# Taps and decays of a long convolution: four blocks in one transfer each, from tables with time on the partitions

## The chip, the cores and the metric

The kernel runs on one core of a Trainium2 chip. The metric is the device time of one execution in microseconds, the median of three runs. The engines are named as in the profile: PE does the matmuls (PEld its weight loads), DVE and POOL elementwise work, ACT activations and copies, SP issues most of the DMAs. SPq and ACTq are the queues' own issuing instructions.

## The reference

Two layers with a residual each. The first is a long convolution along time for each of 512 channels, the second a routed low-rank FFN on the first 4096 tokens (of batch 0).

```python
# x: (8, 4096, 512), float32; N = 16 states for each channel
x = x + conv(_layernorm(x))
x = x + ffn(_layernorm(x))

# conv
p, a = sigmoid(delta), sigmoid(alpha)
q = 1.0 - p * a
kernel = p * beta * jnp.exp(t * jnp.log(q))                     # (512, 16, 4096)
k = jnp.einsum('dnl,dn->dl', kernel, gamma * scale)             # taps, (512, 4096)
out = irfft(rfft(xt, n=2*l) * rfft(k, n=2*l))[..., :l] + x * omega

# ffn: for each expert e, tokens gathered by index, output scattered with weights
h = gelu(xr @ w1A[e].T @ w1B[e]);  ye = h @ w2A[e].T @ w2B[e]
```

## The kernel before

Time is cut into 32 chunks of 128 steps. Within a chunk the convolution is a 128 x 128 triangular Toeplitz matrix for each channel (`local`, L1568), and what earlier chunks add goes through 16 states for each channel (`chunk`, L1553; a scan on DVE, L1380; `between`, L1580). Channels go in **units** of 8 and **blocks** of two units (16 channels, `KD`). There are 32 blocks for each half of the batch, so 64 blocks and 128 units. A **tile** is 8 blocks (128 channels) of 128 rows of x, 8 MB, loaded and stored in 16 pieces.

The span has five parts: the start, in which SP streams x for the layer norm's sums while PE and ACT build tables (0 to 117 us); the first half of the batch (to about 374 us); the FFN (to about 785 us); the second half (to 1047 us); and the last stores.

The **tables** are built at the start, one block at a time (`table`, L948 on ACT and L1531 on PE). For a block, ACT makes two exponentials (L953). PE multiplies them into 4 x 512 numbers of taps, with channel pairs on the partitions and time along the row, and transposes them. ACT copies taps (L961) and decays (L963) out of PSUM and issues a DMA for each (L969, L971) to `decay_d` and `taps_d` in HBM.

In the **blocks**, taps and decays come back block by block. SP's `load_weights` (L777) issues one DMA of 256 KB for the taps (32 partitions, each shifted by one step, eight rows of 256 numbers) and one of 128 KB for the decays. Four blocks of taps lie in `wide`, in four groups of 32 partitions, and four of decays in `dk`. Each pair is issued three blocks ahead, when ACT has turned and POOL has placed the block before the present one (`s_rev`, `s_wd`). Between the pairs SP issues the loads of the next tile and the stores of the last one (`tile`, L800).

ACT's program for a unit is five instructions (`steps`, L1000): an exponential (L1008), a scaled copy of the chunk sums (L1012), two reversals that turn taps in time into the Toeplitz matrix `wb` (L1031, 1024 numbers on each of 32 partitions; L1032, 768), and a copy to the lower partitions (L1038). A row of `wide` holds time with the two channels of a pair side by side, so the reversal reads every second number, backwards: steps of 8 bytes. It writes `wb` without gaps. Only block 0 of the second half is turned by DVE (`reverse2`, L1461), because ACT is in the FFN then.

POOL centres half of a unit (L625) and copies decays to `near` (L574). DVE centres the other half (L1342), scales (L1353), scans (L1380) and adds the result to x (L1364). Each engine runs its program in order, and semaphores count units.

Of the kernel before, what the change touches and what calls it, by code (L numbers as in the profile page):

```python
# [48 lines left out]
def build(nc, x, delta, alpha, beta, gamma, omega, ew, ei, w1a, w1b, w2a, w2b, out, ei_experts=8):  # L49
# [20 lines left out]
    TB = 4  # L70
    WB = 4
    NL = P // LR
# [40 lines left out]
    with ctx:  # L113
# [18 lines left out]
        wide = sb("wide", [P, 2 * UC * P])  # L132
# [17 lines left out]
        om = sb("om", [P, NU, 2])  # L150
        eps = sb("eps", [P, 1])
        root = sb("root", [P, 2])
        lag = sb("lag", [P, 2, 2 * D])
        spare = sb("spare", [P, 4])


# [35 lines left out]
        tok_x = wide[:].rearrange("p (k h d) -> p k h d", k=2, h=2)  # L192
        turned_taps = wide[0:SB // 2, :].rearrange("p (h k i d) -> p h k i d", h=TB, k=2, d=2)
        taps_in = wide[:].rearrange("p (s m) -> p s m", s=SB)
# [13 lines left out]
        out_lag = lag[:].rearrange("p k (h d) -> p k h d", h=2)  # L208
# [4 lines left out]
        carry_row = carry[:].rearrange("p k c -> p (k c)")  # L213
        hot = carry_row[:, 0:3 * E * TT].rearrange("p (k e j) -> p k e j", k=3, e=E)
# [29 lines left out]
        slots_l = lag[0:NSC, 0, 0:2 * P].rearrange("c (p w) -> c p w", w=2)  # L244
# [22 lines left out]
        s_tapd = [sem(f"s_tapd{k}") for k in range(TB)]  # L267
        s_dk = [sem(f"s_dk{k}") for k in range(WB)]
# [9 lines left out]
        s_w = [sem(f"s_wk{k}") for k in range(WB)]  # L278
# [145 lines left out]

        def joined(t):

            return t % DG == 1
# [6 lines left out]
        def _(pool):  # L434
# [8 lines left out]
            const(pool.memset(om[:], 0.0))  # L443
# [124 lines left out]
            def place_decays(i):  # L568

                dst = near[:, i % 2][:, :, 0:3:2, :]  # L570
                src = dk[:, i % WB].rearrange("p (n s d) -> p s d n", s=SB, d=2)
                wait(pool, s_loc, 2 * (i - 1))
                wait(pool, s_dk[i % WB], 16 * (i // WB + 1))
                pool.tensor_copy(dst, src).then_inc(s_wd, 1)  # L574
# [145 lines left out]
        def _(sp):  # L720
# [33 lines left out]
            sp.dma_start(om[0:SB // 2], omega.rearrange("(u s d) -> s u d", d=2, s=SB // 2)).then_inc(s_om, 16)  # L754
# [5 lines left out]
            sp.dma_start(taps_d.rearrange("k s i d -> (k s) i d")[:, P:P + ZR, :]  # L760
                         .rearrange("(a p) i d -> p a (i d)", p=P), zero).then_inc(s_tab, 16)
# [10 lines left out]
            for k in range(TB):  # L772
                sp.wait_ge(s_tapd[k], 16 * (NK // TB))
            sp.wait_ge(s_dec, 16 * NK)
            sp.wait_ge(s_tab, 16)

            def load_weights(i, k):  # L777

                kb = i % NK if isinstance(i, int) else sp.snap(i % NK)
                row = taps_d[bass.ds(kb, 1)].rearrange("k s i d -> k (s i d)")  # L780
                dec = decay_d[bass.ds(kb, 1)].rearrange("k s n d -> (k s) (n d)")
                turned, placed = 2 * (i - WB + 1), i - WB + 1
                now(sp, turned, placed)
                wait(sp, s_rev, turned)
# [3 lines left out]
                wait(sp, s_wd, placed)  # L788
                if isinstance(i, int) and NK <= i < NK + WB:
                    sp.wait_ge(s_dn, grp(NP))  # L790
                sp.dma_start(dk[:, k, :], dec).then_inc(s_dk[k], 16)
# [66 lines left out]
            def tiles(g):  # L858
                t0 = g * DG
                if g == 0:  # L860
                    for k in range(1, WB):
                        load_weights(k, k)
# [53 lines left out]
            for k in range(WB):  # L916
                load_weights(NK + k, k)
# [8 lines left out]
            for k in range(2):  # L926
                sp.wait_ge(s_s[2 * k], 16 * ((NQ + 1 - k) // 2))
                sp.wait_ge(s_s[2 * k + 1], 16 * (NP // 2))
# [6 lines left out]
        def _(act):  # L935
# [20 lines left out]
            def table_copied(i):  # L956
# [3 lines left out]
                wait(act, s_tapd[i % TB], 16 * (i // TB))  # L960
                act.activation(turned_taps[:, i % TB].rearrange("p k i d -> p k d i"),  # L961
                               ps[0:SB // 2, 4 * h, :].rearrange("p (k d i) -> p k d i", k=2, d=2), ACT.Copy)
# [3 lines left out]
            def table_out(i):  # L966

                act.wait_ge(s_cp, i + 1)
                act.dma_start(decay_d[i].rearrange("s n d -> s (n d)"),  # L969
                              decays[:, i].rearrange("p n d -> p (n d)")).then_inc(s_dec, 16)  # L970
                act.dma_start(taps_d[i, :, 0:P, :].rearrange("(k s) i d -> s k (i d)", k=2),  # L971
                              turned_taps[:, i % TB].rearrange("p k i d -> p k (i d)")).then_inc(s_tapd[i % TB], 16)

            act.wait_ge(s_const, NCONST)
            for i in range(NK):
# [3 lines left out]
                if i > 1:  # L979
                    table_out(i - 2)  # L980
            table_copied(NK - 1)
            table_out(NK - 2)
# [808 lines left out]
```

## Time and profile before

| | us |
|---|---|
| median of 3 runs | 1080.95 |
| the runs | 1082.27, 1079.19, 1080.95 |
| the profiled execution | 1070.18 |
| its span, first to last instruction | 1068.0 |
| busy in the span: PE, DVE, ACT, POOL | 869.4, 816.4, 761.4, 571.5 |
| mean granted clock of PE | 0.94 |

The shares of busy time are means over five parts with different limits, so each part is read by itself. The profile's groups give, for a line of the code and a shape, the count, the busy time, the mean duration and the idle time of the engine just before; the waits say what ended such idle time; the timeline gives single instructions.

### The profile page before, as it was taken

The numbers are of one execution on the slowest core, as the hardware profiler recorded it, in microseconds if no ns is written. First come the engines' busy times: TensorE is split into PE (matmuls) and PEld (weight loads), VectorE is DVE, ScalarE is ACT, GpSimd is POOL, SyncE is SP. The second block draws the span as 40 slices with busy tenths as digits, with TensorE's granted clock in tenths as the row PEclk, the third lists the DMA queues.
The fourth block names the chain that finished last, engine by engine and source line by source line (L and its number), as shares of the span: only waits on it lengthen the run. The fifth ranks groups of instructions, "written<-read, shape, count | busy, mean of one in ns | idle before, by whom it ended". The sixth has DMA issues, their size and how long they took to land.

```text
span 1068.0 us, 31991 instructions
## 1 busy us (share of the span) xinstructions
PE 869.4 (81%) x11186; PEld 730.9 (68%) x11186; DVE 816.4 (76%) x1350; ACT 761.4 (71%) x1124; POOL 571.5 (54%) x641
## 2 busy tenths in 40 slices
PE   2770588887868969999999999997878889786981
PEld 1550477776757758888888888886757777675771
DVE  7988899987969834577777777775689998797891
ACT  3882599997969756566665665664459999696990
POOL 5444788867857232666666656655553333332330
PEclk9995699998989979999999999999989999898996
DMA  8999899999999979999999999899669999999977
GB/s 300 351 400 385 211 264 209 271 266 295 308 279 285 327 182 309 257 293 318 286 312 259 242 268 244 246 256 240 174 157 268 226 252 281 287 296 300 295 159 158
DMA packets 390529, 286.11 MB, mean 268 GB/s; under 512 B 124784, under 2 KB 338434, under 8 KB 389948
## 3 DMA queue, kind: packets, MB, share of 16 engines
q1 hardware_dynamic: 345980, 211.67, 72.6%
q0 software_dynamic: 17952, 34.42, 14.6%
q10 hardware_dynamic: 26528, 39.14, 10.4%
q8 instruction: 39, 0.64, 0.3%
q14 instruction: 30, 0.25, 0.1%
HBM read 195.57 MB, written 98.77 MB: 276 GB/s over the span
## 4 chain that ended last, share of the span: by engine, by line
PE 31%; issue 17%; ACT 15%; DVE 14%; DMA 13%; POOL 3%; SPq 2%; DVEq 1%; ACTq 1%; POOLq 0%
PE ps L1688 8%; DMA xb<-L_attn_x 6%; PE ps L1714 6%; ACT wb L1032 6%; DVE xb L1364 4%; ACT wb L1038 4%; PE ps L1562 4%; PE ps L1575 3%; PE ps L1587 3%; DMA wide<-y_d,slot_g 3%; ACT carry L1008 3%; DVE wb L1182 2%; PE ps L1650 2%; PE ps L1663 2%; DVE state L1380 2%
## 5 line engine op out<-in xcount | busy, mean ns | idle before, releaser
L1575 PE MATMUL ps<-xn,wb 128*128 128x128 f32 x2048 | 273.0, 288 | 0.0
L1575 PEld LDWEIGHTS ps<-xn,wb 128*128 128x128 f32 x2048 | 248.0, 198 | 17.0 <-issue 2.3
L625 POOL TENSOR_TENSOR cen<-xb,mean 128x512 f32<-128x512 f32 x128 | 142.8, 1119 | 217.0 <-DVE state L1380 144.2
L1353 DVE TENSOR_TENSOR xn<-cen,rstd 128x1024 f32<-128x1024 f32 x128 | 177.1, 1384 | 44.9 <-POOL cen L625 36.1
L1140 ACT ACTIVATE cen<-ps 128x1024 f32<-128x1024 f32 x110 | 109.2, 1023 | 101.6 <-PE ps L1688 64.7
L1562 PE MATMUL ps<-xn,near 128*32 128x128 f32 x2048 | 87.5, 291 | 113.0 <-DVE xn L1353 67.9
L1364 DVE TENSOR_TENSOR xb<-xb,ps 128x1024 f32 (+1 forms) x128 | 152.7, 1193 | 7.6 <-PE ps L1587 7.6
L1031 ACT ACTIVATE wb<-wide 32x1024 f32<-32x1024 f32 x126 | 144.5, 1147 | 15.4 <-DMA wide<-taps_d 12.9
L1562 PEld LDWEIGHTS ps<-xn,near 128*32 128x32 f32 x2048 | 52.6, 113 | 137.2 <-issue 72.1
L1688 PE MATMUL ps<-carry,wb 64*128 64x256 f32 x1024 | 126.8, 388 | 7.7 <-DVE carry L1426 4.6
L1688 PEld LDWEIGHTS ps<-carry,wb 64*128 64x128 f32 x1024 | 99.4, 190 | 37.1 <-issue 18.5
L1195 DVE BATCH_NORM_STATS2 xb<-xb 128x512 f32 (+1 forms) x128 | 84.3, 684 | 45.3 <-DMA xb<-L_attn_x 45.1
L1032 ACT ACTIVATE wb<-wide 32x768 f32<-32x768 f32 x126 | 114.8, 911 | 1.5
L505 POOL DMA_INDIRECT slot_d<-rowf,posi x64 | 106.1, 1658 | 11.9 <-issue 11.9
L1342 DVE TENSOR_TENSOR cen<-xb,mean 128x512 f32<-128x512 f32 x128 | 90.2, 705 | 9.3 <-DMA xb<-L_attn_x 9.2
L1714 PE MATMUL ps<-cen,xn 128*64 128x128 f32 x1536 | 96.4, 275 | 0.0
L1587 PE MATMUL ps<-state,carry 32*128 32x128 f32 x2048 | 93.6, 297 | 0.0
L1182 DVE BATCH_NORM_STATS2 wb<-xb 128x512 f32 (+1 forms) x128 | 79.8, 681 | 15.7 <-DMA xb<-L_attn_x 14.5
L1714 PEld LDWEIGHTS ps<-cen,xn 128*64 128x64 f32 x1536 | 84.3, 137 | 5.3 <-issue 5.1
L1587 PEld LDWEIGHTS ps<-state,carry 32*128 32x128 f32 x2048 | 69.2, 186 | 25.9 <-issue 25.1
L1038 ACT ACTIVATE wb<-wb 64x512 f32<-64x512 f32 x128 | 80.5, 629 | 4.9 <-DVE wb L1466 1.8
L1008 ACT ACTIVATE carry<-far,rate 128x384 f32<-128x384 f32 x128 | 79.0, 617 | 3.2
(211 smaller groups left out, 1311.4 us busy)
## 6 DMA issues: line engine op xcount, KB each, us to landing
xb<-L_attn_x SPq DMA_DIRECT2D x160, 512.0 KB, 7.4
out<-xb SPq DMA_DIRECT2D x72, 512.0 KB, 6.4
xb<-L_attn_x ACTq DMA_DIRECT2D x128, 256.0 KB, 5.8
out<-xb SPq DMA_DIRECT2D x88, 256.0 KB, 4.7
wb<-L_ffn_w_B SPq DMA_DIRECT2D x78, 256.0 KB
wide<-taps_d SPq DMA_DIRECT2D x63, 256.0 KB, 5.8
dk<-decay_d SPq DMA_DIRECT2D x63, 128.0 KB, 5.6
out<-y_d SPq DMA_DIRECT2D x4, 1536.0 KB, 11.6
```

The lines of the kernel that those rows point to most:

```text
L625: pool.tensor_tensor(cen[:, k, 0:QB // 2].rearrange("p b r d -> p r b d"), unit_view(pool, g, i, k)[:, :, 0:UC // 2] .rearrange("p r (b d) ...
L1008: act.activation(carry[:, k, 0:CR + P], far[:], ACT.Exp, scale=rate[:, bass.ds(col, 1)])\
L1031: act.activation(dst[0:ZR], src, ACT.Copy)
L1032: act.activation(dst[ZR:2 * ZR, :, :, ZR:P], src[:, :, :, 0:P - ZR], ACT.Copy).then_inc(s_rev, 1)
L1038: act.activation(taps[2 * ZR:P, :, :, 2 * ZR:P], taps[0:2 * ZR, :, :, 0:2 * ZR], ACT.Copy)\
L1353: dve.tensor_tensor(xn[:, k].rearrange("p (b d) r -> p b d r", d=2), cen[:, k].rearrange("p b r d -> p b d r"), rstd[:, g * P:(g + 1) * P] ...
L1364: dve.tensor_tensor(view, view, ps[:, QB * k:QB * k + QB, 0:2 * P] .rearrange("p b (d r) -> p r b d", d=2), ALU.add).then_inc(s_ev, 1)
L1562: ins = pe.matmul(ps[b * 2 * N:(b + 1) * 2 * N, QB * k, 2 * P:3 * P], near[:, h, k * QB + b, d:d + 2, :].rearrange("p z n -> p (z n)"), xn ...
L1575: ins = pe.matmul(ps[:, QB * k + b, d * P:(d + 1) * P], wb[:, h, k * QB + b, d, :], xn[:, k, 2 * b + d, :], start=(b > 0 and d == 0), stop ...
L1587: ins = pe.matmul(ps[:, QB * k + b, d * P:(d + 1) * P], carry[rows, k, d * P:(d + 1) * P], state[rows, k, :], start=False, stop=True, skip ...
L1688: ins = pe.matmul(ps[:, 2 * (b % 2) + h, f * QT:(f + 1) * QT].rearrange("p (a t) -> p a t", a=2), w1bs[half_rows, k, c * P:(c + 1) * P], r ...
L1714: ins = pe.matmul(ps[h * RANK:(h + 1) * RANK, 4, 0:P], w2as[:, (f // 2) * (FC // 2) + 2 * b + f % 2, :], act_at(q, b)[:, f, side * P:(side ...
```

## The change

Taps in HBM are now laid out as `taps_d[block, time, 16 channels]`, decays as `decay_d[group of four blocks, state, 4 x 256]`. On PE the roles in the table's matmul are swapped: the exponential is the stationary operand and the 8 coefficient columns move, so the result has time on 128 partitions and 16 channels along the row. ACT's copy of the taps is 128 x 16 in place of 4 x 512. The DMAs that write the tables are issued once for four blocks.

One DMA now loads the taps of four blocks: 128 partitions, each one run of 2048 numbers (8 KB), 1 MB in all. One loads their decays, 512 KB. Both have two buffers: `taps_in[:, 0:2]`, the second half of which is the old `lag` buffer, and `dk` with `dk_odd` (inside `carry`). SP still waits for `s_rev` and `s_wd` at each block, since its other DMAs are paced by them, but issues taps and decays twice for each tile.

A row of `taps_in` holds time with 16 channels side by side. The reversal on ACT reads one channel of them backwards in time: its innermost step is 16 numbers, 64 bytes. It writes `wb` as before, and its instructions have the shapes that they had.

Because `lag` holds the FFN's last results until the scatter has read them, SP waits for all scatters (`scattered`) before the first load into it in the second half.

```diff
-        taps_d = nc.dram_tensor("taps_d", [NK, SB, P + ZR, 2], F32).ap()
-        decay_d = nc.dram_tensor("decay_d", [NK, P, N, KD], F32).ap()
+        taps_d = nc.dram_tensor("taps_d", [NK, P + ZR, KD], F32).ap()
+        decay_d = nc.dram_tensor("decay_d", [NG, P, WB * N * KD], F32).ap()
...
+        def taps_of(q, n, k):
+            return taps_in[q * ZR:(q + 1) * ZR, n, :].rearrange("p (i c) -> p i c", c=KD)[:, ::-1, k * UC:(k + 1) * UC]\
+                .rearrange("p m (s d) -> p s d m", d=2)
...
-                src = bass.AP(row.tensor, row.offset, [[2, ZR], [2 * (P + ZR), SB], [1, 2 * P]])
-                sp.dma_start(taps_in[k * ZR:(k + 1) * ZR], src).then_inc(s_w[k], 16)
...
+            def load_taps(n, k0=0):
+                wait(sp, s_rev, 2 * WB * (n - 1))
+                wait(sp, s_w, 16 * n)
+                first = taps_d[n % NG * WB + k0]
+                src = bass.AP(first.tensor, first.offset, [[(P + ZR) * KD, WB - k0], [KD, ZR], [1, P * KD]])
+                sp.dma_start(taps_in[k0 * ZR:, n % 2, :], src).then_inc(s_w, 16)
...
-                        load_weights(t * BT + b + WB - 1, (b + WB - 1) % WB)
+                        wait(sp, s_rev, 2 * (t * BT + b))
+                        wait(sp, s_wd, t * BT + b)
+                    if b == (1 if first else 0):
...
+                        load_taps(2 * t + 1)
+                        load_decays(2 * t + 1)
+                    elif b == WB and not final:
+                        load_taps(2 * t + 2)
+                        load_decays(2 * t + 2)
...
             def reverse(i, k, m):
-                src = taps_in[m * ZR:(m + 1) * ZR, k * QB:(k + 1) * QB].rearrange("p s (m d) -> p s d m", d=2)[:, :, :, ::-1]
+                src = taps_of(m % WB, m // WB, k)
...
-                    for d in range(2):
-                        pe.matmul(o[:, k, d, :], own_coef[:, u, d::2], decay[:, 2 * h + k, :],
-                                  start=(k == 0 and d == 0), stop=False, skip_group_check=True)
+                    pe.matmul(ps[:, 4 * h, k * UC:(k + 1) * UC], decay[:, 2 * h + k, :], own_coef[:, u, :],
+                              start=(k == 0), stop=False, skip_group_check=True)
```

Two places show the order. The first is SP at the end of the second tile of the first half: pieces of the next tile are loaded (`xb<-L_attn_x`), taps and decays of coming blocks fetched. Before:

```order
L732 DMA xb<-L_attn_x 128x8x128
L787 DMA wide<-taps_d 32x8x256
L791 DMA dk<-decay_d 128x256
L851 DMA out<-xb 128x8x64
L732 DMA xb<-L_attn_x 128x8x128 x4
L787 DMA wide<-taps_d 32x8x256
L791 DMA dk<-decay_d 128x256
L787 DMA wide<-taps_d 32x8x256
L791 DMA dk<-decay_d 128x256
L749 DMA y_d<-xb 128x8x128 x4
```

and with the change:

```order
L886 DMA out<-xb 128x8x64
L750 DMA xb<-L_attn_x 128x8x128
L886 DMA out<-xb 128x8x64
L750 DMA xb<-L_attn_x 128x8x128 x4
L801 DMA taps_in<-taps_d 128x1x2048
L807 DMA carry<-decay_d 128x1024
L767 DMA y_d<-xb 128x8x128 x4
L750 DMA xb<-L_attn_x 128x8x128
```

Three pairs of DMAs have become one pair of four blocks' size, and the four loads of x no longer stand behind one.

The second is ACT in the first unit of a half. Before:

```order
L1008 ACTIVATE carry<-far,rate 128x384
L1012 ACTIVATE shift_s<-ps,coef 128x4x31
L1031 ACTIVATE wb<-wide 32x1024
L1032 ACTIVATE wb<-wide 32x8x96
L1038 ACTIVATE wb<-wb 64x8x64
```

and with the change:

```order
L1035 ACTIVATE carry<-far,rate 128x384
L1039 ACTIVATE shift_s<-ps,coef 128x4x31
L1061 ACTIVATE wb<-taps_in 32x1024
L1062 ACTIVATE wb<-taps_in 32x8x96
L1068 ACTIVATE wb<-wb 64x8x64
```

Nothing moves: the same five instructions of the same shapes stand in the same order, with other names and line numbers (L1061 and L1062 are the reversals). The loop over them is written for eight blocks in place of four.

## Rows read from the trace of the kernel before

**Rows 1.** Groups of ACT's instructions, 120 to 374 us: busy, mean ns, idle before.

```profile
L1031 ACT ACTIVATE wb<-wide 32x1024 f32<-32x1024 f32 x62 | 71.2, 1149 | 1.4
L1032 ACT ACTIVATE wb<-wide 32x768 f32<-32x768 f32 x62 | 56.5, 912 | 0.7
L1038 ACT ACTIVATE wb<-wb 64x512 f32<-64x512 f32 x63 | 39.6, 629 | 1.5
L1008 ACT ACTIVATE carry<-far,rate 128x384 f32<-128x384 f32 x63 | 38.9, 617 | 1.6
L1012 ACT ACTIVATE shift_s<-ps,coef 128x124 f32<-128x124 f32 x64 | 22.7, 355 | 23.6 <-PE ps L1562 23.2
```

**Rows 2.** The same groups, 785 to 1047 us.

```profile
L1012 ACT ACTIVATE shift_s<-ps,coef 128x124 f32<-128x124 f32 x64 | 22.7, 355 | 25.3 <-PE ps L1562 24.6
```

**Rows 3.** Windows: PE, PEld, DVE, ACT, POOL busy (instructions), granted clock, DMA, GB/s.

```profile
140.00:160.00 20.00, 17.89 (x254) 15.21 (x252) 18.80 (x23) 19.53 (x28) 17.87 (x14) 1.00 1.10 258
...
740.00:760.00 20.00, 14.01 (x172) 11.97 (x171) 12.78 (x30) 6.98 (x11) 11.47 (x11) 0.91 1.03 260
```

**Rows 4.** Waits of ACT, 120 to 374 us: total, times, longest.

```profile
ACT shift_s L1012 <- PE ps L1562: 23.2, 10, 7.9
```

**Rows 5.** Waits of ACT, whole span.

```profile
ACT wb L1031 <- DMA wide<-taps_d: 12.9, 1, 12.9
```

**Rows 6.** Groups of all engines, whole span.

```profile
L574 POOL COPY near<-dk 128x256 f32<-128x256 f32 x64 | 40.2, 628 | 0.0
...
L1083 ACT ACTIVATE xn<-ps 128x512 f32<-128x512 f32 x64 | 34.8, 595 | 4.3 <-PE ps L1650 4.2
...
L497 POOL COPY xb<-xb 128x256 f32<-128x256 f32 x64 | 25.4, 403 | 41.3 <-DMA xb<-L_attn_x 40.5
...
L963 ACT ACTIVATE xb<-ps 128x256 f32<-128x256 f32 x32 | 18.3, 573 | 0.0
...
L1120 ACT ACTIVATE xb<-wb 128x256 f32 x39 | 16.3, 417 | 49.1 <-PE ps L1663 24.3 <-DVE xb L1208 17.1 <-issue 6.7
...
L1226 DVE TENSOR_TENSOR rstd<-rstd 128x128 f32<-128x128 f32 x2 | 0.6, 286 | 0.0
...
L1228 DVE TENSOR_TENSOR rstd<-rstd,xb 128x128 f32<-128x128 f32 x1 | 0.4, 387 | 0.0
```

**Rows 7.** One line's instructions, L1465 and L1466: ns min/median/max.

```profile
L1465 DVE COPY wb<-wide x2: 681/1882/3084, 782.9 to 786.6; 32x1024 f32<-32x1024 f32 x2
...
L1466 DVE COPY wb<-wide x2: 549/549/549, 786.0 to 787.3; 32x768 f32<-32x768 f32 x2
```

**Rows 8.** Timeline at the tile boundary, 229 to 247 us: start, us, engine, instruction, [idle].

```profile
229.32 6.67 SPq L732 DMA_DIRECT2D xb<-L_attn_x  x4
...
234.18 0.64 PE L1562 MATMUL ps<-xn,near 128*32 128x128 f32 x16 [0.17 <-DVE xb L1364]
...
235.41 2.05 PE L1575 MATMUL ps<-xn,wb 128*128 128x128 f32 x16
...
237.39 0.73 PE L1587 MATMUL ps<-state,carry 32*128 32x128 f32 x16
...
242.30 1.59 POOL L625 TENSOR_TENSOR cen<-xb,mean 128x512 f32<-128x512 f32 x1 [9.67 <-DMA xb<-L_attn_x]
...
245.36 1.08 PE L1562 MATMUL ps<-xn,near 128*32 128x128 f32 x16 [7.24 <-DVE xn L1353]
...
246.37 3.78 PE L1575 MATMUL ps<-xn,wb 128*128 128x128 f32 x16
...
246.60 0.36 ACT L1012 ACTIVATE shift_s<-ps,coef 128x124 f32<-128x124 f32 x1 [7.93 <-PE ps L1562]
```

**Rows 9.** Timeline of ACT before the first blocks, 109 to 116 us.

```profile
114.88 0.40 ACT L997 ACTIVATE rstd<-var,eps 128x128 f32<-128x128 f32 x1 [13.54 <-DVE var L1230]
```

**Rows 10.** DMA issues, section 6 of the page: KB each, us to landing.

```profile
wide<-taps_d SPq DMA_DIRECT2D x63, 256.0 KB, 5.8
```

**Rows 11.** Timeline of the end, 1024 to 1068 us.

```profile
1045.48 1.22 DVE L1364 TENSOR_TENSOR xb<-xb,ps 128x1024 f32<-128x1024 f32 x1 [1.42 <-PE ps L1587]
```

More of the change, by code:

```diff
@@ L266, in build @@
         s_dec = sem("s_dec")
-        s_tapd = [sem(f"s_tapd{k}") for k in range(TB)]
-        s_dk = [sem(f"s_dk{k}") for k in range(WB)]
+        s_tapd = sem("s_tapd")
+        s_dk = sem("s_dk")
+        s_first = sem("s_first")
+        s_dkf = sem("s_dkf")
         s_wd = sem("s_wd")
@@ L277, in build @@
         s_x = sem("s_x")
-        s_w = [sem(f"s_wk{k}") for k in range(WB)]
+        s_w = sem("s_w")
         s_cen = sem("s_cen")
@@ L771, in _, with load_decays, scattered @@
             sp.wait_ge(s_keep, NL)
-            for k in range(TB):
-                sp.wait_ge(s_tapd[k], 16 * (NK // TB))
-            sp.wait_ge(s_dec, 16 * NK)
+            sp.wait_ge(s_tapd, 16 * NG)
+            sp.wait_ge(s_dec, 16 * NG)
             sp.wait_ge(s_tab, 16)
[L777 to L784, printed above, removed]
-                src = bass.AP(row.tensor, row.offset, [[2, ZR], [2 * (P + ZR), SB], [1, 2 * P]])
-                sp.dma_start(taps_in[k * ZR:(k + 1) * ZR], src).then_inc(s_w[k], 16)
[L788 to L791, printed above, removed]
+            def load_taps(n, k0=0):
[4 more added lines that the diff above has]
+                sp.dma_start(taps_in[k0 * ZR:, n % 2, :], src).then_inc(s_w, 16)
+            def load_decays(n, k0=0):
+                wait(sp, s_wd, WB * (n - 1))
+                wait(sp, s_dk, 16 * n)
+                sp.dma_start(dk_of[n % 2][:, k0:], decay_d[n % NG, :, k0 * N * KD:]
+                             .rearrange("p (k c) -> p k c", k=WB - k0)).then_inc(s_dk, 16)
+            def scattered():
+                for k in range(2):
+                    sp.wait_ge(s_s[2 * k], 16 * ((NQ + 1 - k) // 2))
+                    sp.wait_ge(s_s[2 * k + 1], 16 * (NP // 2))
             def in_turn(n):
@@ L860, in tiles @@
                 if g == 0:
-                    for k in range(1, WB):
-                        load_weights(k, k)
+                    load_taps(0, 1)
+                    load_decays(0, 1)
                 tile(g, t0, True, False)
@@ L915, in _ @@
             sp.wait_ge(s_a, NQ)
-            for k in range(WB):
-                load_weights(NK + k, k)
+            load_taps(NG)
+            sp.wait_ge(s_dn, grp(NP))
+            load_decays(NG)
             sp.wait_ge(s_dv, 2 * DV_STATS)
@@ L1007, in steps @@
                     wait(act, s_pe, QB * (u - 1))
-                    act.activation(carry[:, k, 0:CR + P], far[:], ACT.Exp, scale=rate[:, bass.ds(col, 1)])\
+                    act.activation(grow[:, k, :], far[:], ACT.Exp, scale=rate[:, bass.ds(col, 1)])\
                        .then_inc(s_ca, 1)
@@ L1027, in reverse @@
                 dst = wb[:, m % 2, k * QB:(k + 1) * QB]
-                src = taps_in[m * ZR:(m + 1) * ZR, k * QB:(k + 1) * QB].rearrange("p s (m d) -> p s d m", d=2)[:, :, :, ::-1]
-                wait(act, s_w[m], 16 * (i // WB + 1))
+                src = taps_of(m % WB, m // WB, k)
+                if isinstance(i, int) and i == 0:
+                    act.wait_ge(s_first, 16)
+                else:
+                    wait(act, s_w, 16 * (i // WB + 1))
                 wait(act, s_loc, 2 * (i - 1))
@@ L1039, in lower, with over_groups @@
                    .then_inc(s_low, 1)
-            def over_quarters(g):
+            def over_groups(g):
+                n = 2 * WB
                 steps(g * NK, 0, True, False)
-                with act.Fori(g * NK // WB, (g + 1) * NK // WB - 1) as p:
-                    for m in range(1, WB + 1):
-                        steps(p * WB + m, m % WB, False, False)
-                for m in range(1, WB):
-                    steps((g + 1) * NK - WB + m, m, False, m == WB - 1)
+                with act.Fori(g * NK // n, (g + 1) * NK // n - 1) as p:
+                    for m in range(1, n + 1):
+                        steps(p * n + m, m % n, False, False)
+                for m in range(1, n):
+                    steps((g + 1) * NK - n + m, m, False, m == n - 1)
             act.wait_ge(s_late, NLATE)
@@ L1379, in steps @@
                     wait(dve, s_pe, QB * (u - 1))
-                    dve.tensor_tensor_scan(state[:, k, :], carry[:, k, CR:CR + P],
+                    dve.tensor_tensor_scan(state[:, k, :], grow[:, k, CR:CR + P],
                                            shift_s[:, k].rearrange("p b c -> p (b c)"), 0.0,
@@ L1586, in between @@
                         rows = slice(b * 2 * N, (b + 1) * 2 * N)
-                        ins = pe.matmul(ps[:, QB * k + b, d * P:(d + 1) * P], carry[rows, k, d * P:(d + 1) * P],
+                        ins = pe.matmul(ps[:, QB * k + b, d * P:(d + 1) * P], grow[rows, k, d * P:(d + 1) * P],
                                         state[rows, k, :], start=False, stop=True, skip_group_check=True)
```

98 lines of the change are left out of this document (52 added, 46 removed).

## The prediction

> **What bounds the kernel now.** I read the span by its parts first. The change touches the start, the two halves with the blocks (120 to 374 us and 785 to 1047 us) and the seam between FFN and second half; the FFN and the last stores do the same work as before. In the blocks the windows come next. In 20 us of them ACT is busy for 19.53, DVE for 18.80, PE for 17.89 at a granted clock of 1.00, and the DMA share is 1.10 [rows 3]. So ACT is the fullest engine. Its groups say why: in one unit it runs 617 + 355 + 1149 + 912 + 629 = 3662 ns [rows 1], and 128 units of that are 469 us of the span's 1068. Then its waits, to see what ends last. Within the first half ACT is idle for 23.2 us before L1012, in 10 waits of up to 7.9 us [rows 4], and 24.6 in the second [rows 2]; nearly all of it lies at the tile boundaries. There the timeline shows POOL held for 9.67 us by a load of x whose queueing began at 229.32, and ACT then held for 7.93 [rows 8]. For taps from HBM ACT waits once in the whole span, 12.9 us in the start [rows 5], and never in the blocks. The two lessons: a longer ACT instruction in the blocks costs its full length 126 times, and an earlier tap costs or gives nothing there.
>
> **The change, part by part.**
>
> *Transfers.* A 256 KB load of taps lands 5.8 us after issue [rows 10] and is issued three blocks ahead, which is 6 x 3.66 = 22 us. That is hidden now and stays hidden with 1 MB loads issued four blocks ahead, and the second buffer removes a wait that isn't there [rows 5]. What fewer issues can give is only the boundary: the four last loads of x no longer stand behind a pair. That is bounded by the boundary waits, 47.8 us in all [rows 2, 4]. The Trainium skill (DMA: Bandwidth & Descriptors, Rules for kernel authors) advises to coalesce many small transfers into one large one, since each pays a fixed cost; by that rule this change gains. The rows agree that the queue is full, but show the cost of these transfers itself behind other work.
>
> *Reversals on ACT.* The two instructions keep their shapes, but read at steps of 64 bytes instead of 8. No ACT instruction of this trace reads SBUF so, therefore I bound it. ACT's copies without gaps give the base: 629 ns for 512 numbers [rows 1] and 417 for 256 [rows 6] are 0.83 ns a number and 204 ns fixed. The reversals of now are at (1149 - 912) / 256 = 0.93 ns a number, so a step of 8 bytes is nearly free. For long steps there are three neighbours. ACT writing at 64 bytes (L963): 256 numbers take 573 ns; L1083, 512 numbers without gaps from PSUM, takes 595, so 256 would take 382: 0.75 ns more a number. POOL reading at 64 bytes (L574) takes 628 against 403 without gaps (L497): 0.88 more a number. DVE reading one operand at 24 bytes (L1228) takes 387 against 286 (L1226): 0.79 more [rows 6]. Three engines, reading and writing, pay 0.75 to 0.88 ns, about one clock, for each number at steps of 24 or 64 bytes. The nearest is ACT's own row and POOL's for the same step, so I take their middle, one more clock of ACT, 0.83 over its base. The unit's 1792 numbers then take 2 x 204 + 1792 x 1.66 = 3383 ns instead of 2061: **+1.32 us a unit**. Low end 0.75: 3239, +1.18. High end, today's 0.93 doubled: 3741, +1.68. An end at zero is the first rival.
>
> The Trainium skill (SBUF — State Buffer, Specifications and the note on cachelines) says that SBUF is read in lines of 16 bytes and that full speed needs two hits on each. Now there are two numbers of a channel pair on a line, with the change one. By that page the change costs; the neighbours' rows agree with it, and only for ACT's reading it is untested.
>
> The unit on ACT becomes 3.66 + 1.32 = 4.98 us. PE's work in one is 0.64 + 2.05 + 0.73 = 3.42 us [rows 8], and DVE, at 18.80 of 20, has less than ACT now. So ACT sets the pace, and no other engine comes near. 126 units are turned on ACT, 62 of them in the stretch of [rows 1]. The first two are turned in the start, ahead of 13.54 us in which ACT waits for the variances [rows 9]; their 2.6 us are covered, and would show if those 13.54 were gone. The other 124 pay: **124 x 1.32 = +164 us** (ends 146 and 208).
>
> *What comes back.* A tile's 16 units take 80 us instead of 59 plus the boundary wait, while its loads and stores move the same bytes. The queue that is full now gets some 12 us of slack for each tile, and the loads of x that end the boundary waits land nearly in time. Now four of them are queued over 6.67 us from 229.32 and let POOL go at 242.30, 13 us on [rows 8]; with room in the queue this shrinks towards the 5.8 us in which a transfer of 256 KB lands [rows 10] and a little for the issues, while the need for them comes later. Of the 47.8 us I keep 2 to 3 for each of six boundaries and a few at the ends: **-30 us** (ends -40 and -20).
>
> *The seam.* DVE turns block 0 of the second half with the other engines waiting. Now the four copies run at (681 - 549) / 256 = 0.52 ns a number [rows 7]. A long step at least doubles this, and may add 0.79 to that: 3584 numbers x 0.52 to 1.3 = 1.9 to 4.7 us. I take **+3**.
>
> *The start.* ACT's table copies of 4 x 512 shrink to 128 x 16, and 64 DMAs to 16. ACT waits 13.54 us afterwards [rows 9] and DVE's sums of x end this part, so it is hidden: 0. *SP's wait for the scatters* in the second half holds the first loads of the next tile by some 14 us of a tile that lasts 80; the load has the rest of it: 0. *The end:* the last addition starts at 1045.48 [rows 11], and 21 us of stores follow as before.
>
> The sum against the profiled execution: 1070 + 164 - 30 + 3 = 1207 us. The median of the runs is 10.8 us above that execution (1080.95 against 1070.18), and I carry this over, less a little because ACT now covers the queue: **1216 us**.
>
> **The rivals.**
>
> *No price for the step* (faster). ACT might read ahead and not feel it. Then the pace stays 3.66 us and only the boundaries change: at most 47.8 us less, more likely 5 of some 8 us at each of six: 1081 - 30 = 1051 us, seen between 1035 and 1075. For it: no row shows ACT reading with a long step. Against: three neighbours, and the 0.10 ns that even the 8 byte step costs ACT.
>
> *The clock falls* (far slower). With ACT at 4.98 us PE is idle for 1.6 us of each unit instead of 0.2. At a boundary, after 7.24 us without work, its matmuls ran at the lower level: 1.08 and 3.78 us where 0.64 and 2.05 stand at the higher [rows 8]. With those, and L1587 longer in the same measure (0.73 to about 1.3), PE needs 6.1 us a unit, is the bound instead of ACT, and adds 124 x 1.1 = 137 us: about 1350. Against: the window from 740 us, with PE busy for 14.01 of 20, had a granted clock of 0.91 [rows 3], and the new pauses are short.
>
> *It does nothing*: the step is free, and the boundaries don't move because the bytes of x bound them, not the issues. Then 1081, within 0.3%.
>
> **How the numbers follow.** Reversals that pay: 87%. Free step with a gain: 8%. Clock falls: 3%. Nothing: 2%. The forecast is the first, 1216. Its ends: 1070 + 146 - 40 + 2 + 11 = 1189 and 1070 + 208 - 20 + 5 + 11 = 1274. The 13% of the others stay outside, and the range is 1188 to 1272. Faster by over 0.3% (what a measurement of this kernel can tell from no change): 0.08. Within: 0.02. Slower: 0.90.
>
> **What would show it.** The group of the first reversal at 1.9 us (1.74 to 2.1) and of the second at 1.48; ACT busy for over 19 of 20 us in the blocks while DVE and PE fall to about 14; 5.0 us from one L1353 to the next; ACT's waits in the halves down to some 10 us each; granted clock at 1.00 in the blocks; the start's end within 2 us of now. If the first reversal shows 1.15 us, the forecast is wrong at its main step and the boundaries decide. If it shows 1.9 and the time rises by less than 120 us, the waits gave back more than I allow, or another engine's slack was no slack.

## The result and the profile after

The changed kernel takes 1278.89 us (median of 4 runs, 1277.67 to 1283.65) against 1080.33 for the kernel before in the same set of runs (1079.19 to 1082.27). The ratio is 1.186, with a 95% interval of 1.1825 to 1.1892: 198.6 us slower. The forecast was 1216, its range 1188 to 1272. The direction was right; the time lies 7 us above the range and 63 above the forecast. The profiled execution took 1283.65 us, its span 1281.5. Here and below a ratio leaves out runs that lie over 1.5% above the fastest of their kernel, which are two of the twelve of e8 and no others.

Of the profile after, first ACT's groups from 120 to 450 us, which answer to [rows 1] (busy us, mean ns of one, idle us before and what ended it):

```profile
L1061 ACT ACTIVATE wb<-taps_in 32x1024 f32<-32x1024 f32 x60 | 117.0, 1951 | 11.2 <-DMA taps_in<-taps_d 10.1
L1062 ACT ACTIVATE wb<-taps_in 32x768 f32<-32x768 f32 x59 | 90.8, 1540 | 0.7
L1068 ACT ACTIVATE wb<-wb 64x512 f32<-64x512 f32 x59 | 37.1, 628 | 1.4
L1035 ACT ACTIVATE carry<-far,rate 128x384 f32<-128x384 f32 x59 | 36.3, 616 | 1.5
L1039 ACT ACTIVATE shift_s<-ps,coef 128x124 f32<-128x124 f32 x60 | 20.8, 346 | 20.1 <-PE ps L1591 20.1
```

Three of the five instructions last what they lasted; the two reversals went from 1149 to 1951 and from 912 to 1540 ns, +1.43 us a unit. The last line shows a second thing. ACT is still idle for 20.1 us before L1039, where it was 23.2 [rows 4], though with a longer unit over half of that was to go.

The windows (columns as in [rows 3]; the first two in the blocks, the next two in the seam between FFN and second half):

```profile
140.00:160.00 20.00, 16.39 (x208) 13.80 (x211) 13.88 (x17) 19.66 (x21) 11.01 (x11) 0.87 0.54 132
200.00:250.00 50.00, 33.48 (x480) 27.88 (x480) 34.93 (x41) 49.24 (x51) 30.27 (x26) 1.00 0.81 193
...
896.00:900.00 4.00, 0.00 (x0) 0.00 (x0) 0.00 (x0) 0.22 (x2) 0.00 (x0) 0.53 0.25 66
900.00:906.00 6.00, 0.00 (x0) 0.00 (x0) 0.00 (x0) 0.00 (x0) 0.00 (x0) 0.50 0.24 81
```

Where the blocks run undisturbed, ACT is busy for 49.24 of 50 us and bounds them as forecast. In the seam's windows all engines stand still, one load of taps and one of decays are under way, and yet the DMA share is 0.25 and 0.24. Sixteen engines at 0.25 are four at full use; that it is four is an inference here, which e7 tests. What happened there, in the timeline (start, us, engine, instruction, [idle]):

```profile
888.35 0.65 SPq L801 DMA_DIRECT2D taps_in<-taps_d  x1
889.10 0.37 SPq L807 DMA_DIRECT2D dk<-decay_d  x1
...
906.74 1.01 DVE L1496 COPY wb<-taps_in 32x1024 f32<-32x1024 f32 x1 [13.37 <-DMA taps_in<-taps_d]
907.77 0.79 DVE L1497 COPY wb<-taps_in 32x768 f32<-32x768 f32 x1
...
907.91 1.12 POOL L592 COPY near<-dk 128x256 f32<-128x256 f32 x1 [15.72 <-DMA dk<-decay_d]
...
908.59 0.63 ACT L1068 ACTIVATE wb<-wb 64x512 f32<-64x512 f32 x1 [12.36 <-DVE wb L1497]
```

The 1 MB of taps are there 18 us after their issue, where 256 KB took 5.8 [rows 10], and DVE, POOL and ACT stand still for 12 to 16 us. The decays, issued right behind, land with them. The page's DMA issues show that for the whole span (KB each, us to landing; before, 128 KB of decays took 5.6):

```profile
carry<-decay_d SPq DMA_DIRECT2D x8, 512.0 KB, 20.4
```

Within the blocks ACT waits for the taps themselves once for long (10.1 us, in the first of them), but the queue stands still behind each load. The second tile boundary of the first half, which answers to [rows 8]:

```profile
257.89 0.53 SPq L801 DMA_DIRECT2D taps_in<-taps_d  x1
...
259.63 15.35 SPq L886 DMA_DIRECT2D out<-xb  x1
...
290.25 4.78 SPq L750 DMA_DIRECT2D xb<-L_attn_x  x4
...
301.61 1.59 POOL L643 TENSOR_TENSOR cen<-xb,mean 128x512 f32<-128x512 f32 x1 [17.94 <-DMA xb<-L_attn_x]
...
305.91 0.36 ACT L1039 ACTIVATE shift_s<-ps,coef 128x124 f32<-128x124 f32 x1 [12.20 <-PE ps L1591]
```

The taps are issued at 257.89, a store behind them holds SP's queue for 15.35 us, and the four last loads of the next tile go out at 290.25 only. That the store is held by the load of taps is not shown by this trace; e3 tests it. POOL is held for 17.94 us and ACT for 12.20, where it was 9.67 and 7.93. The waits over the whole span (total, times, longest):

```profile
POOL cen L643 <- DMA xb<-L_attn_x: 92.3, 16, 21.2
ACT shift_s L1039 <- PE ps L1591: 51.5, 9, 13.9
ACT wb L1061 <- DMA taps_in<-taps_d: 26.9, 3, 15.6
...
DVE wb L1496 <- DMA taps_in<-taps_d: 13.4, 1, 13.4
```

Why four engines? The source of this DMA is written as `[[(P + ZR) * KD, WB - k0], [KD, ZR], [1, P * KD]]`, whose outermost dimension is the number of blocks: 4. The source of the old 256 KB load had 32 (`ZR`) there. The Trainium skill (DMA: Bandwidth & Descriptors, Why a DMA increments its semaphore by 16 and not by 1) states that a DMA runs on the largest number of engines, up to 16, that divides the slowest dimension of source and destination; with 4 and 128 that is 4. The trace's 0.25 agrees with it. The same page's advice to coalesce was weighed in the prediction; this rule, which speaks against the change as written, was not.

### The profile page after: what moved, and what is told of

Same layout as the page of the kernel before. It is cut to its first block and busy times, and to the rows that moved or that the text cites. A ratio compares the mean times of both kernels' runs of the same rounds, so it can differ in the third digit from the quotient of the medians.

```text
span 1281.5 us, 31550 instructions
## 1 busy us (share of the span) xinstructions
PE 931.2 (73%) x11058; PEld 789.6 (62%) x11058; DVE 819.4 (64%) x1350; ACT 925.0 (72%) x1124; POOL 565.8 (44%) x641
## 5 line engine op out<-in xcount | busy, mean ns | idle before, releaser
L1604 PE MATMUL ps<-xn,wb 128*128 128x128 f32 x2048 | 304.6, 310 | 121.1 <-ACT wb L1068 120.5
L1604 PEld LDWEIGHTS ps<-xn,wb 128*128 128x128 f32 x2048 | 278.8, 219 | 146.2 <-ACT wb L1068 142.9
L1061 ACT ACTIVATE wb<-taps_in 32x1024 f32<-32x1024 f32 x126 | 245.8, 1951 | 29.3 <-DMA taps_in<-taps_d 26.9
L1384 DVE TENSOR_TENSOR xn<-cen,rstd 128x1024 f32<-128x1024 f32 x128 | 172.1, 1344 | 61.0 <-POOL cen L643 32.2
L1062 ACT ACTIVATE wb<-taps_in 32x768 f32<-32x768 f32 x126 | 194.0, 1540 | 1.5
L1171 ACT ACTIVATE cen<-ps 128x1024 f32<-128x1024 f32 x110 | 109.4, 1024 | 97.2 <-PE ps L1717 44.1
L1411 DVE TENSOR_TENSOR_SCAN state<-carry,shift_s 128x128 f32<-128x128 f32 x128 | 54.3, 424 | 152.7 <-ACT shift_s L1039 152.7
L520 POOL DMA_INDIRECT slot_d<-rowf,posi x64 | 99.4, 1553 | 11.9 <-issue 11.9
L1743 PE MATMUL ps<-cen,xn 128*64 128x128 f32 x1536 | 99.4, 275 | 0.0
L1068 ACT ACTIVATE wb<-wb 64x512 f32<-64x512 f32 x128 | 80.4, 628 | 15.4 <-DVE wb L1497 12.4
L1743 PEld LDWEIGHTS ps<-cen,xn 128*64 128x64 f32 x1536 | 87.0, 137 | 5.5 <-issue 5.4
```

The costliest lines, as they stand in the source:

```text
L520: pool.indirect_dma_start(out=slot_d, out_offset=bass.IndirectOffsetOnAxis(ap=pos_col[:, c:c + 1], axis=0), in_=row_col[:, 2 * c:2 * c + 2 ...
L1061: act.activation(dst[0:ZR], src, ACT.Copy)
L1062: act.activation(dst[ZR:2 * ZR, :, :, ZR:P], src[:, :, :, 0:P - ZR], ACT.Copy).then_inc(s_rev, 1)
L1171: act.activation(act_at(q, b).rearrange("p f t -> p (f t)"), ps[:, 2 * (b % 2):2 * (b % 2) + 2, :].rearrange("p a t -> p (a t)"), ACT.Gelu ...
L1384: dve.tensor_tensor(xn[:, k].rearrange("p (b d) r -> p b d r", d=2), cen[:, k].rearrange("p b r d -> p b d r"), rstd[:, g * P:(g + 1) * P] ...
L1604: ins = pe.matmul(ps[:, QB * k + b, d * P:(d + 1) * P], wb[:, h, k * QB + b, d, :], xn[:, k, 2 * b + d, :], start=(b > 0 and d == 0), stop ...
```

## The experiments

Two causes were on the table after this: the step of 64 bytes on ACT (**A**), and the group loads on four DMA engines (**B**). Runs that are compared with each other shared a chip and their runs of the kernel before: e1 to e4 (1072.55 us median for before), e5, e7 and e8 (1072.00), e9 and e10 (1071.60). The changed kernel itself was run in another set (1080.33 for before), so it is compared with them by ratios. In e1, e2, e4, e5 and e8 the reversals read other places of the buffer than the layout calls for, so the Toeplitz matrices hold other numbers; counts and shapes are as they were.

### e1: the step alone

```diff
-                src = taps_in[m * ZR:(m + 1) * ZR, k * QB:(k + 1) * QB].rearrange("p s (m d) -> p s d m", d=2)[:, :, :, ::-1]
+                src = wide[m * ZR:(m + 1) * ZR, :].rearrange("p (i c) -> p i c", c=KD)[:, ::-1, k * UC:(k + 1) * UC]\
+                    .rearrange("p m (s d) -> p s d m", d=2)
```

> The kernel before, with its own tables, transfers and buffers; only ACT's two reversals read the same quarter of wide at a step of 64 bytes (as rows of 16 numbers), so that the Toeplitz matrices hold other numbers than they should. Theory 1 (the step costs ACT nearly one clock for each number, and transfers are a matter of their own): the first reversal takes 1.95 us and the second 1.54, a unit on ACT 5.09 us instead of 3.66, 124 units x 1.43 = 177 us more, less some 30 us of the boundary waits, since the loads of x are as before: 1215 to 1240 us. Rival (the reversals are slow in the changed kernel because its 1 MB loads write the rows that ACT reads, or because of the address of the buffer): 1.15 and 0.91 us, and 1081 us.

Measured: 1212.44 us (1210.95 to 1215.56), ratio 1.1317 (1.1231 to 1.1404), +140 us, and 3 us under the range expected. The groups and ACT's wait at the boundaries:

```profile
L1032 ACT ACTIVATE wb<-wide 32x1024 f32<-32x1024 f32 x126 | 245.5, 1948 | 15.2 <-DMA wide<-taps_d 12.7
L1033 ACT ACTIVATE wb<-wide 32x768 f32<-32x768 f32 x126 | 193.7, 1537 | 1.5
```

```profile
ACT shift_s L1012 <- PE ps L1563: 17.1, 8, 4.5
```

A alone gives the reversals their new length, to 3 ns, and costs 140 us. The boundary waits fall from 47.8 us [rows 2, 4] to 17.1, with loads and queue as before. 124 units x 1.43 = 177, less 30.7, is 146: the prediction's sum with measured terms, within 6 us of the time.

### e2: the step undone, all else changed

```diff
-            return taps_in[q * ZR:(q + 1) * ZR, n, :].rearrange("p (i c) -> p i c", c=KD)[:, ::-1, k * UC:(k + 1) * UC]\
-                .rearrange("p m (s d) -> p s d m", d=2)
+            return taps_in[q * ZR:(q + 1) * ZR, n, :].rearrange("p (s m d) -> p s m d", s=SB, d=2)[:, k * QB:(k + 1) * QB]\
+                .rearrange("p s m d -> p s d m")[:, :, :, ::-1]
```

> The changed kernel, all of it, except that ACT's and DVE's reversals read the rows of taps_in at a step of 8 bytes (as pairs, as before), which gives other numbers than they should. Theory 1: reversals at 1.15 and 0.91 us. Theory 2 (the 1 MB loads of taps run on 4 of the 16 DMA engines, since their source's slowest dimension is 4, and hold the SP queue for 15 us twice in each tile): with compute at 3.66 us a unit a tile has 59 us of compute and the loads of x come late at every boundary, so the time stays far above before: 1110 to 1170 us. Rival to theory 2 (the long boundary waits come only from the slower pace of the blocks): 1050 to 1085 us.

Measured: 1232.75 us (1227.51 to 1240.7), ratio 1.1505 (1.1402 to 1.1608). Without the step the changed kernel is still 15% slower than before, 63 us above the upper end that I had expected. Its waits:

```profile
ACT shift_s L1039 <- PE ps L1591: 121.2, 24, 24.6
...
POOL near L592 <- DMA dk<-decay_d: 60.3, 6, 15.7
```

```profile
L1061 ACT ACTIVATE wb<-taps_in 32x1024 f32<-32x1024 f32 x126 | 144.2, 1145 | 88.9 <-DMA taps_in<-taps_d 86.5
```

At a unit of 3.7 us the queue has no slack [rows 3], and now ACT waits for the taps themselves too, for 86.5 us.

### e3 and e10: four DMAs of 32 partitions for each group load

The main lines of the edit; the counts that ACT and DVE wait for follow the new number of DMAs:

```diff
-                wait(sp, s_w, 16 * n)
-                first = taps_d[n % NG * WB + k0]
-                src = bass.AP(first.tensor, first.offset, [[(P + ZR) * KD, WB - k0], [KD, ZR], [1, P * KD]])
-                sp.dma_start(taps_in[k0 * ZR:, n % 2, :], src).then_inc(s_w, 16)
+                wait(sp, s_w, 64 * n - 16)
+                for q in range(k0, WB):
+                    first = taps_d[n % NG * WB + q]
+                    src = bass.AP(first.tensor, first.offset, [[KD, ZR], [1, P * KD]])
+                    sp.dma_start(taps_in[q * ZR:(q + 1) * ZR, n % 2, :], src).then_inc(s_w, 16)
```

The same bytes to the same places at the same point of the program. What differs is that there are four DMAs for one, and that each source has 32 outermost in place of 4.

> The changed kernel, all of it and with the right numbers, but the taps of a group are loaded by four DMAs of 256 KB (three the first time), each with 32 as its source's slowest dimension, with the same 8 KB runs and the same double buffer. Theory 2: ahead of the second half, where nothing else moves, the loads take all engines and land within 6 us instead of 18; SP's pauses of 15 us after each load vanish; ACT's waits for taps in the first block go from 10 us to under 3; the time falls by 13 us at the seam, 10 at the first block and 20 to 40 at the boundaries: 1215 to 1240 us, where the prediction was. Rival (runs of 8 KB are slow by themselves, or 1 MB at once is too much for the queue): 1279 us within 5.

Measured: 1213.51 us (1212.5 to 1224.3), ratio 1.1358 (1.1258 to 1.1457), against 1.186 for the changed kernel: under the range expected by 1.5 us, and far from the rival's 1279. In a later job, as e10:

> The kernel of e3 once more, unchanged, to have it in the same job as e9: 1210 to 1218 us, a ratio of 1.126 to 1.146 to the kernel before.

Measured: 1214.74 us (1209.51 to 1221.35), ratio 1.1348 (1.1308 to 1.1388). The issues and waits of e3:

```profile
taps_in<-taps_d SPq DMA_DIRECT2D x63, 256.0 KB, 4.9
```

```profile
ACT shift_s L1040 <- PE ps L1592: 16.9, 8, 4.1
ACT wb L1062 <- DMA taps_in<-taps_d: 15.3, 1, 15.3
DVE wb L1497 <- DMA taps_in<-taps_d: 1.9, 1, 1.9
```

The three waits that had grown are small again: 51.5 to 16.9 us, 26.9 to 15.3 (the one wait in the start, 12.9 before), 13.4 to 1.9. SP's queue no longer stands behind the load. At the same point of the program, where the store took 15.35 us and the one load of x after it 5.24:

```profile
231.24 1.71 SPq L802 DMA_DIRECT2D taps_in<-taps_d  x4
...
233.94 0.58 SPq L887 DMA_DIRECT2D out<-xb  x1
234.57 4.62 SPq L750 DMA_DIRECT2D xb<-L_attn_x  x1
```

So the group load on four engines is what held the store. B costs the changed kernel 0.050 of the ratio, 54 us by the time of before, give or take 11 by the two intervals. The difference of the two medians is 65, but they come from two sets, whose kernels before lie 8 us apart.

### e4: both undone

e3 with the reversals of e2.

> The changed kernel with both: reversals that read at a step of 8 bytes (other numbers than they should) and four DMAs for the taps of a group. What is left of the change is the tables' making, the double buffer and fewer issues. Theory 1 and 2 together: no loss is left, 1050 to 1085 us; below 1077 if fewer issues shorten the boundary waits, as the first rival of the prediction has it (1051). If a third cost of the change exists, for instance in the start or in the wait for the scatters, it shows here as a time above 1085.

Measured: 1080.49 us (1077.38 to 1089.52, 10 runs), ratio 1.0079 (1.0041 to 1.0117). So A and B are the two causes, but for 8 us. That fewer issues shorten the boundary waits did not show: ACT's come to 56.5 us, where they were 47.8. In one job A costs 140 us alone (e1 against before) and 133 on top of four DMAs (e3 against e4). B costs 152 us where the step is short (e2 against e4) and some 54 where it is long. They are not added. My reading, which no run separates, is that both take up the same slack: a queue that stands still for 15 us is covered in part by a unit of 5.0 us and by hardly anything at 3.7. What remains of e4 is seen in its waits: SP's queue for the scatters, and ACT at one boundary. (The profiled execution is e4's slowest, 9 us above its median.)

```profile
ACT shift_s L1040 <- PE ps L1592: 56.5, 21, 18.0
...
SPq L814 <- DMA out<-taps_in,slot_s: 14.0, 1, 14.0
```

### e7: two DMAs of two blocks each

e3 alone leaves another reading: that smaller DMAs are faster, whatever their shape. In this run each DMA has half the size and, by cause B, half the engines. The lines that it adds, waits of ACT and DVE apart:

```diff
+                wait(sp, s_w, 32 * n)
+                for q0, q1 in ((k0, 2), (2, WB)):
+                    first = taps_d[n % NG * WB + q0]
+                    src = bass.AP(first.tensor, first.offset, [[(P + ZR) * KD, q1 - q0], [KD, ZR], [1, P * KD]])
+                    sp.dma_start(taps_in[q0 * ZR:q1 * ZR, n % 2, :], src).then_inc(s_w, 16)
```

> The changed kernel, in which a load of four blocks of taps is two DMAs of two blocks each (64 partitions, 512 KB). Everything else is as changed, and the numbers are right. Theory (the outermost dimension of the DMA's source says how many of the 16 DMA engines it runs on): each of these has 2 there, so it runs on two engines; if both take the same two, 1 MB takes over 30 us and the time goes well above the changed kernel's 1279, to 1300 to 1400 us; if each takes two of its own, 18 us as now and the same 1279. Rival (what counts is how large a DMA is, smaller ones being faster): the time lies between four DMAs and one, 1215 to 1275 us.

Measured: 1360.33 us (1355.3 to 1367.49), ratio 1.270 (1.2636 to 1.2763). One DMA gives 1.186, two give 1.270, four give 1.136, so the size is not it. The time lies in the range expected of two shared engines and 85 us above that of the rival. The seam's windows, where nothing but the loads runs:

```profile
918.00:928.00 10.00, 0.00 (x0) 0.00 (x0) 0.00 (x0) 1.05 (x2) 0.00 (x0) 0.60 0.13 39
928.00:938.00 10.00, 0.00 (x0) 0.00 (x0) 0.00 (x0) 0.00 (x0) 0.00 (x0) 0.50 0.12 52
```

A share of 0.12 to 0.13 is two engines of 16: the two DMAs, 1.2 us apart, shared the same two. DVE waits for 22.3 us there, until 27 after the issue (over 30 was expected).

```profile
938.59 1.02 DVE L1497 COPY wb<-taps_in 32x1024 f32<-32x1024 f32 x1 [22.31 <-DMA taps_in<-taps_d]
```

The changed kernel has a third case in it. Its very first group load is of three blocks (`WB - k0` is 3, 768 KB), issued at 113.59 us and waited for by ACT until 132.84. In between the DMA share is 0.18 to 0.21 until 127 us, and three engines of 16 are 0.19:

```profile
124.00:127.00 3.00, 2.76 (x42) 2.25 (x41) 1.62 (x3) 0.00 (x0) 1.70 (x2) 1.00 0.18 55
```

So 4, 3 and 2 in the outermost place go with shares of 0.25, 0.18 and 0.12.

### e8 and e9: the scatter wait a block later

```diff
-                    if b == (1 if first else 0):
+                    if b == ((2 if g else 1) if first else 0):
```

This was made in e4 (e8) and in e3 (e9).

> The kernel of e4 (four DMAs for each load of taps, ACT's reversals at the old step of 8 bytes, so the matrices hold other numbers), in which the first group load of the second half, with its wait for the scatters, is issued one block later, behind four more loads of x. Question: is SP's wait for the scatters what keeps that kernel 8 us above the kernel before. Theory: it is; the first boundary wait of the second half, 18 to 20 us in e4, falls to under 10, and the time to 1066 to 1074 us, within 0.4% of the kernel before in this job. Rival (the 8 us come from elsewhere, the start or the boundaries' bytes): no change from a ratio of 1.008 to the kernel before.

Measured: 1077.04 us (1067.91 to 1086.25, 12 runs), ratio 1.0014 (0.9986 to 1.0043), where e4 had 1.0079. ACT's longest boundary wait falls from 18.0 to 11.9 us and their sum from 56.5 to 49.3; POOL's wait at that boundary, from 20.3 to 14.2 us, is not under the 10 expected, and neither is the time within the 1066 to 1074. With all twelve runs the ratio of the means is 1.003, and for e4 it is 1.009. So the wait for the scatters is part of e4's 8 us, by these numbers 5 to 7 of them; the two intervals touch, and how much it is isn't settled.

> The kernel of e3 (the changed kernel with four DMAs for each load of taps, ACT's reversals at 64 bytes, right numbers), in which the first group load of the second half, with its wait for the scatters, is issued one block later, behind four more loads of x. The same edit took the kernel at the old step from a ratio of 1.008 to the kernel before to 1.001. Theory: with a unit of 5.0 us the queue has slack, the wait for the scatters costs nothing, and the time is that of e3 in this job within 0.3%. Rival (the wait costs the same at either pace): 5 to 8 us less than e3.

Measured: 1214.65 us (1208.86 to 1218.1) against 1214.74 for e10, ratios 1.1327 and 1.1348 with intervals that overlap. At 5.0 us a unit the wait costs nothing that can be measured.

### e5: eight steps in one run

The kernel before, in which the reversals of four blocks read `wide` with eight different steps. It ran once, and its time as a whole says nothing here; the instructions do. The lines that make the source; `c` is the step in numbers, `j` how many rows of the eight lie one behind the other:

```diff
+                    s = row[:, 0:j * P * c].rearrange("p (j i c) -> p j c i", j=j, c=c)[:, :, 0:8 // j, :]
+                    s = s[:, :, :, ::-1] if back else s
```

> The kernel before, in which the eight pairs of reversals of four blocks read the taps buffer with eight different steps between the numbers, into the same places as before: backwards at 4, 8, 12, 16, 24, 32 and 64 bytes, and forward at 8. The matrices then hold other numbers; shapes, writes and counts are as before. Question: is the price a matter of the step's length, and from where on. My theory after the first runs: a number costs one clock of ACT more as soon as its step is longer than a line of 16 bytes holds, so 4 and 8 bytes take about 1150 ns for 1024 numbers, 16 bytes and more take 1850 to 1950 alike, and 12 bytes lie between, at 1.4 to 1.9 us; the direction costs nothing. Rival (the price grows with the step, as a distance would): 16 bytes at about 1.25 us, 32 at 1.45, 64 at 1.95.

Measured, over the whole span, in this order: steps of 4, 8, 12, 16 and 64 bytes, each with 1024 and 768 numbers a partition.

```profile
L1042 ACT ACTIVATE wb<-wide 32x1024 f32<-32x1024 f32 x15 | 15.6, 1041 | 13.1 <-DMA wide<-taps_d 13.1
L1043 ACT ACTIVATE wb<-wide 32x768 f32<-32x768 f32 x15 | 12.6, 843 | 0.2
L1054 ACT ACTIVATE wb<-wide 32x1024 f32<-32x1024 f32 x16 | 18.4, 1150 | 0.4
L1055 ACT ACTIVATE wb<-wide 32x768 f32<-32x768 f32 x16 | 14.5, 909 | 0.2
L1046 ACT ACTIVATE wb<-wide 32x1024 f32<-32x1024 f32 x15 | 24.1, 1607 | 0.0
L1047 ACT ACTIVATE wb<-wide 32x768 f32<-32x768 f32 x15 | 18.9, 1258 | 0.2
L1058 ACT ACTIVATE wb<-wide 32x1024 f32<-32x1024 f32 x16 | 33.3, 2084 | 0.4
L1059 ACT ACTIVATE wb<-wide 32x768 f32<-32x768 f32 x16 | 25.9, 1619 | 0.2
L1070 ACT ACTIVATE wb<-wide 32x1024 f32<-32x1024 f32 x16 | 31.9, 1991 | 0.4
L1071 ACT ACTIVATE wb<-wide 32x768 f32<-32x768 f32 x16 | 24.8, 1549 | 0.2
```

The difference of each pair, over 256 numbers, is the price of one number free of what is fixed:

| step, bytes | 4 | 8 | 8, forward | 12 | 16 | 24 | 32 | 64 |
|---|---|---|---|---|---|---|---|---|
| 1024 numbers, ns | 1041 | 1150 | 1150 | 1607 | 2084 | 2014 | 2132 | 1991 |
| 768 numbers, ns | 843 | 909 | 906 | 1258 | 1619 | 1568 | 1650 | 1549 |
| ns a number | 0.77 | 0.94 | 0.95 | 1.36 | 1.82 | 1.74 | 1.88 | 1.73 |

The price is full at 16 bytes and does not grow from there, so the rival with a price that grows with the distance falls. My own numbers were off in two places: 4 bytes are cheaper than 8 (1041 against 1150 ns), and from 16 bytes on 1024 numbers take 1991 to 2132 ns, not 1850 to 1950. Direction costs nothing. Up to 16 bytes the price fits how many lines of 16 bytes a number opens: a quarter of 1.82 is below the 0.77 of the dense copy, a half of it is 0.91 (0.94 measured), three quarters 1.37 (1.36). The sweep doesn't explain the spread of 1.73 to 1.88 from 16 bytes on, nor why a number at 64 bytes took (1951 - 1540) / 256 = 1.61 ns in the changed kernel and in e1, and 1.73 here, where only the order of the dimensions outside the step differs. The Trainium skill (SBUF — State Buffer, Specifications and the note on cachelines) speaks of lines of 16 bytes and of two hits on each for full speed. That the price rises between 8 and 16 bytes agrees with it; that two hits give full speed does so only nearly, since 8 bytes took 0.94 ns and 4 bytes 0.77.

## Why the prediction was right in part and wrong in its size

**What bounds the blocks:** right. ACT is busy for 49.24 of 50 us, DVE and PE are busy for two thirds, and units come every 5.0 us.

***Transfers*, the step that failed.** It said that a load is "hidden now and stays hidden with 1 MB loads issued four blocks ahead", and the sum has no term for it. Two things were wrong in it. The 5.8 us of [rows 10] were carried over to a DMA whose source has another shape; the new one takes 18 to 19 us. And the step asked only who waits for these bytes. In the changed kernel ACT does so three times, 26.9 us in all, of which 12.9 were there before [rows 5], but the loads of x stand behind them, and e3 puts the price of the whole at 54 us. The diff had what was needed: the old source begins with `[2, ZR]`, which is 32, and the new one with `WB - k0`, which is 4. The prediction read the lengths of this DMA and not its order of dimensions. That "the four last loads of x no longer stand behind a pair" was so in the order, and worthless: they stand behind the pair's stall.

***Reversals*:** right in the mechanism, and 0.11 us a unit too low, 14 us over 124 units. It was +1.43 us a unit against 1.32 forecast, inside the ends of 1.18 and 1.68. 1951 and 1540 ns stand against 1.9 and 1.48 us. The price of a number was well placed: 1.61 ns by the difference of the two lengths against 1.66. What is fixed was not: 1951 - 1024 x 1.61 leaves some 305 ns for each instruction, where the sum had 204.

***What comes back*:** right where B is absent. 30.7 us in e1 against 30 forecast; e3 shows 16.9 us of waits left. In the changed kernel, with 51.5 us, nothing came back.

***The seam*:** +3 was forecast for slower copies on DVE. The four took 4.76 us (1.01, 0.79, 1.35 and 1.60) and cost nothing, since the four of before took 4.86: the 1882 of [rows 7] is the middle of 681 and 3084, and the first copy was the long one, beside a centring on POOL. Before, on DVE and ACT:

```profile
782.89 3.08 DVE L1465 COPY wb<-wide 32x1024 f32<-32x1024 f32 x1
...
786.58 0.63 ACT L1038 ACTIVATE wb<-wb 64x512 f32<-64x512 f32 x1 [1.76 <-DVE wb L1466]
```

The slope was as forecast: 0.88 ns a number for 0.52. The load cost the seam instead: ACT stood for 12.4 us before L1068, where it had stood for 1.8 before L1038.

***The start*:** 0 was forecast. The variances' end came 2.5 us later (117.37 for 114.88 [rows 9], where 2 were allowed), 1.1 in e3; for this I have no cause. In addition ACT waited for 10.1 us at 132.84, for the first group load, which e3 takes away and which belongs to B.

***SP's wait for the scatters*:** 0 was forecast for a tile of 80 us, and e9 shows it. At the old pace the same wait costs some 5 to 7 us (e4, e8); the step held because it was argued from the new pace.

***The end*:** as before. The last addition starts at 1258.93, 22.6 us before the end of the span; before, it was 22.5 [rows 11].

**The sum.** With B away the prediction's 1216 stands beside 1213.5 and 1214.7 in e3 and e10, but that it comes so near is in part luck: the kernel before was 8 to 9 us faster in those jobs. By ratios, 1216 is 1.125, e3 and e10 are 1.136 and 1.135, and the changed kernel is 1.186. So B is 0.050 of the miss of 0.061. The rest, some 11 us, has the size of what the reversals were short by (14). The warning in the prediction's last part was written for it ("another engine's slack was no slack"), but only for a time that was too short.

**The rivals.** A free step is excluded by e1, and e4 and e8 show no gain from fewer issues. The fall of the clock, put at 3% against a forecast of 1.00 in the blocks, did come for parts of them, also in e1 and e3, where no load of taps holds the queue. Two windows, from the changed kernel and from e3 (columns as in [rows 3]):

```profile
170.00:180.00 10.00, 8.19 (x107) 6.87 (x100) 6.70 (x9) 9.84 (x10) 5.74 (x6) 0.83 1.17 265
```

```profile
210.00:220.00 10.00, 8.03 (x96) 6.82 (x96) 6.56 (x9) 9.83 (x11) 5.60 (x6) 0.83 1.13 296
```

A granted clock of 0.83 is a mean of both levels: in windows of 2 us of e3 (212 to 220 us) it went between 0.50 and 1.00. PE had been busy for 6.5 us of 10 at 1.00 before it fell (180 to 190 us of e3), and was busy for 8.0 to 8.3 at 0.83, by my estimate 4.1 us of a unit's 5.0. That is not the 6.1 of the rival, so ACT stayed the bound, busy for 9.83 of 10 at either clock. The forecast held because there was room under ACT's pace, not because the clock did.

No version was found that beats the kernel before. Even with both costs removed e8 stands at 1.0014, and no run removes the step with right numbers. The best forms of the change with right numbers are e3, e10 and e9, at 1.133 to 1.136.

## What to carry to other kernels

When loads are merged, read the merged DMA's shape and not only its bytes: an outermost dimension of 4 where there were 32 put the load on a quarter of the engines. And ask who is queued behind a transfer as well as who waits for it; here the taps themselves were late for ACT and DVE in three places (10.1, 13.4 and 1.3 us), and the loads of x behind them held POOL for 92.3 us in all, where it is 52.2 in e3. A layout that makes a transfer easy is paid for where it is read: 16 channels side by side cost ACT 1.43 us for each unit, on the engine that bounds the loop, for a transfer that was hidden.

## What the runs showed of the hardware

- A DMA of 1 MB whose source's outermost dimension is 4 kept the DMA share at 0.25 and took 18 us; two of 512 KB with 2 there kept it at 0.12 to 0.13 and took 27 us together, so they ran on the same engines; one of 768 KB with 3 there went with 0.18 and 19 us. Four of 256 KB with 32 there landed in 4.9 us each (median).
- DMAs issued behind such a load were late with it: 512 KB of decays landed in 20.4 us (7.9 in e4, with the taps as four DMAs), and a store held SP's queue for 15.35.
- ACT reads numbers of 4 bytes at 0.77 ns (dense), 0.94 (8 bytes), 1.36 (12 bytes) and 1.73 to 1.88 (16 to 64 bytes) each; backwards is as fast as forwards.
- DVE's copy at 64 bytes took 0.88 ns a number against 0.52 at 8.
- PE's granted clock fell to a mean of 0.83 for 40 us at a time in blocks (e1 from 160, e3 from 190 us) in which PE had been busy for 6.5 to 6.7 us of 10; ACT, which bounds the loop, stayed busy for 9.83 of 10.
